# TensorE's side work in front of the flips of probabilities in an attention loop

## The chip, the cores and the metric

The kernel runs on one core of one Trainium2 chip. The metric is the device time of one execution in microseconds (us).

## The reference, cut to what matters

Four batches of 512 tokens with 512 features go through a small cross attention, an attention block with a mixture of 8 experts, a second cross attention and a second mixture of 32 experts. The attention block, in which the change lies, computes for normed x of shape 4 x 512 x 512:

```
kv_d, q_d = x @ kv_d_w, x @ q_d_w                    # 512 -> 128
k_p, q_p, v = kv_d @ k_u_w, q_d @ q_u_w, kv_d @ v_u_w
k_r, q_r = rope(x @ rope_k_w), rope(q_d @ rope_q_w)
k, q = concat(k_p, k_r), concat(q_p, q_r)            # 16 heads of 32
probs = softmax(causal(q @ k.T / sqrt(32)))
h = x + (probs @ v) @ o_w
```

Then `rmsnorm(h)` goes to a router (7 logits a token, two experts chosen) and to the first mixture.

## The kernel before

The function `front` holds the attention block. Each engine has its own program, written out in order by hand; they meet only through semaphores. A loop over 128 steps n (four batches b of 32 steps s) does the attention. A step is one pair of heads and one tile of 128 queries. Steps 0 to 15 of a batch take query tiles 1 and 0 in turn, with 256 and 128 keys (narrow steps); steps 16 to 31 take tiles 3 and 2, with 512 and 384 keys (wide steps). A narrow step is one unit with both heads, `(n, None)`; a wide step is two units, `(n, 0)` and `(n, 1)`, one head each. There are 192 units.

For a unit, TensorE computes the scores (L1092) and adds the causal mask (L1093); VectorE takes the row maxima (`maxima`, L869); ScalarE takes the exponentials (`exponents`, L739); TensorE transposes these probabilities block by block (`flip_probs`, L1134) into PSUM bank 4, or bank 5 for a second head of a wide step; bank 4 is copied to `prob_t` by VectorE (`prob_t_first`, L876) and bank 5 by ScalarE (`prob_t_second`, L748); TensorE multiplies with the values for two steps at a time (`attend`, L1112). TensorE runs the scores two units ahead. `take(bank, name, n)` makes TensorE wait until the last user of a PSUM bank has been copied out, in program order of the `take` calls.

With each step goes a piece of work for the neighbouring batches, `between(b, s)`, on TensorE, ScalarE and VectorE alike. For the batch to come: flips of its normed input and the down projections (steps 0 to 4), `plain` (L1154, L1155), `turned` (L1160, L1162) and `values` (L1168) for token tiles 0 and 1 at steps 6 to 8 and for tiles 2 and 3 at steps 14, 15 and 18 to 21, and the flips of queries and keys (L1082) at steps 9, 12 and 22 to 28. VectorE rotates the result of `turned` (`rotate`, L933 to L940) and forms the low parts of queries and keys (L917, L923); ScalarE copies the results out (L764, L770, L777, L782). For the batch done: the output projection (`output`, L1185; steps 0, 1, 3, 5), flips of its normed rows (steps 10, 11, 13) and the router's `logits` (L1198; steps 12, 14, 15). In the last batch, steps 20 and 24 hold an `output` of that batch itself. Steps 16, 17, 23, 25 and 27 have nothing for TensorE.

The order of work that matters here: TensorE does, for each unit, scores of the unit two ahead, `attend`, flips of denominators, the flip of this unit's probabilities, then `between`. VectorE does maxima of the next unit, then the copy of the last flip and the last step's `between`. ScalarE does this unit's exponentials, then the copy of the last second-head flip and the last step's `between`.

Of the kernel before, what the change touches and what calls it, by code (L numbers as in the profile page):

```python
# [42 lines left out]
NS = len(STEPS)  # L43
# [500 lines left out]
def front(nc, a, m, c, dram, s_init):  # L544
    ctx = ExitStack()
    with ctx:
# [70 lines left out]
        def copied_first(n):  # L617

            b, s = divmod(n, NS)
            return b * (NS + PHASE) + (s + 1 + min(s + 1, PHASE))  # L620

        def copied_second(n):
            b, s = divmod(n, NS)
            return b * PHASE + max(0, s + 1 - PHASE)
# [444 lines left out]
        def _(pe):  # L1069
# [4 lines left out]
            def take(bank, name, n):  # L1074

                if bank in emptied and emptied[bank] != (name, n):
                    pe.wait_ge(S[emptied[bank][0]], emptied[bank][1])
                emptied[bank] = (name, n)
# [44 lines left out]
            def flip_probs(n, e):  # L1123
                i, u = STEPS[n % NS][0], n % 2
                bank = 5 if e == 1 else 4
                pe.wait_ge(S["pexp"], 2 * n + heads_of(n, e)[-1] + 1)
                if e == 1:
                    take(5, "ptb", copied_second(n))
                else:
                    take(4, "pta", copied_first(n))  # L1130
                for e in heads_of(n, e):
                    for j in range(i + 1):
                        at = block_of(n, e, j) % TPB * P
                        last = tr(ps[:, bank, at:at + P], prob[:, u, e, j * P:(j + 1) * P], ident)  # L1134
                last.then_inc(S["pt"], 1 if is_wide(n) else 2)

            def z_flip(b, t):
                pe.wait_ge(S["z"], b * TPB + t + 1)
                take(BANK["zt"][t], "zts", b * TPB + t + 1)
                four(BANK["zt"][t], z[:, t, :]).then_inc(S["zt"], 1)  # L1140

            def down(b, w, name, out, bank):
                pe.wait_ge(S["zts"], TPB * (b + 1))
                take(bank, out, b + 1)
                for k in range(DC):
                    last = mm(ps[:, bank, :], w[:, k, :], z_t[:, k, :], start=(k == 0), stop=(k == DC - 1))
                last.then_inc(S[name], 1)

            def plain(b, t):
                q, bank = slice(t * P, (t + 1) * P), BANK["pp"][t]  # L1150
                pe.wait_ge(S["kvds"], b + 1)
                pe.wait_ge(S["qds"], b + 1)
                take(bank, "qkp", b * TPB + t + 1)
                mm(ps[:, bank, 0:256], q_d[:, q], w_q[:, 0:256], start=True, stop=True)  # L1154
                mm(ps[:, bank, 256:512], kv_d[:, q], w_ku[:, :], start=True, stop=True).then_inc(S["pp"], 1)  # L1155

            def turned(b, t):
                q = slice(t * P, (t + 1) * P)
                take(3, "qkr", b * TPB + t + 1)
                mm(ps[:, 3, 0:256], q_d[:, q], w_q[:, 256:512], start=True, stop=True)  # L1160
                for k in range(DC):
                    last = mm(ps[:, 3, 256:512], z_t[:, k, q], w_kr[:, k, :], start=(k == 0), stop=(k == DC - 1))  # L1162
                last.then_inc(S["pr"], 1)

            def values(b, t):
                pe.wait_ge(S["kvds"], b + 1)
                take(BANK["v"][t], "vs", b * TPB + t + 1)
                mm(ps[:, BANK["v"][t], :], kv_d[:, t * P:(t + 1) * P], w_vu[:, :], start=True, stop=True).then_inc(S["pv_"], 1)  # L1168

            def queries_flip(b, t):  # L1170
                pe.wait_ge(S["qkp"], b * TPB + t + 1)
                pe.wait_ge(S["qkr"], b * TPB + t + 1)
                take(BANK["tq"][t], "qls", b * TPB + t + 1)
                four(BANK["tq"][t], qk[:, t % 2, 0:HEADS, :].rearrange("p h e -> p (h e)")).then_inc(S["tq"], 1)

            def keys_flip(b, t):
                take(BANK["tk"][t], "kls", b * TPB + t + 1)
                four(BANK["tk"][t], qk[:, t % 2, HEADS:2 * HEADS, :].rearrange("p h e -> p (h e)")).then_inc(S["tk"], 1)

            def output(b, n):  # L1180
                t, bank = QUERY_ORDER[n], OUT_BANK(b, n)
                pe.wait_ge(S["attd"], b * TPB + n + 1)
                take(bank, "hres", b * TPB + n + 1)
                for k in range(DC):
                    last = mm(ps[:, bank, :], att_t[:, t, k, :], w_o[:, k, :], start=(k == 0), stop=(k == DC - 1))  # L1185
                last.then_inc(S["oproj"], 1)

            def hidden_flip(b, t):
                pe.wait_ge(S["hn"], b * TPB + t + 1)
                take(BANK["hnt"][t], "hnts", b * TPB + t + 1)  # L1190
                four(BANK["hnt"][t], h[:, t, :]).then_inc(S["hnt"], 1)
# [9 lines left out]
            def ranks(b):  # L1201
                pe.wait_ge(S["masked"], b + 1)
                take(3, "slotted", b + 1)
                places(nc, r, MOE0, c, m, m["before0"], 3).then_inc(S["ranked"], 1)

            def between(b, s):

                done, then = b - 1, b + 1
                if then < BATCH and s in (0, 1):
                    z_flip(then, 2 * s)  # L1210
                    z_flip(then, 2 * s + 1)
                if done >= 0:
                    if s in (0, 1):
                        output(done, s)
                    if s in (3, 5):
                        output(done, (s + 1) // 2)
                if then < BATCH:
                    if s == 2:
                        down(then, w_kvd, "kvd", "kvds", BANK["kvd"])
                    if s == 4:  # L1220
                        down(then, w_qd, "qd", "qds", BANK["qd"])
                    if s in (6, 7):
                        plain(then, s - 6)
                    if s in (6, 8):
                        turned(then, s // 2 - 3)
                        values(then, s // 2 - 3)
                    if s in (9, 12):
                        queries_flip(then, s // 3 - 3)
                        keys_flip(then, s // 3 - 3)
                if done >= 0:  # L1230
                    if s == 10:
                        hidden_flip(done, 0)
                    if s == 11:
                        hidden_flip(done, 1)
                        hidden_flip(done, 2)
                    if s == 12:
                        logits(done, 0)
                        logits(done, 1)
                    if s == 13:
                        hidden_flip(done, 3)  # L1240
                    if s in (14, 15):
                        logits(done, s - 12)
                if then < BATCH:
                    if s in (14, 15):
                        values(then, s - 12)
                    if s in (18, 20):
                        plain(then, s // 2 - 7)
                    if s in (19, 21):
                        turned(then, s // 2 - 7)
                    if s in (22, 26):  # L1250
                        queries_flip(then, s // 4 - 3)
                    if s in (24, 28):
                        keys_flip(then, s // 4 - 4)
                if b == LAST and s in (20, 24):
                    output(LAST, s // 4 - 5)
                if done >= 0 and s == 30:
                    ranks(done)
# [17 lines left out]
            for at in range(len(UNITS) + 4):  # L1275
                if at + 2 < len(UNITS):
                    n, e = UNITS[at + 2]
                    for e in heads_of(n, e):
                        scores(n, e)
                if at >= 2 and at - 2 < len(UNITS):  # L1280
                    n, e = UNITS[at - 2]
                    if n % 2 == 1 and e != 0:
                        attend(n - 1)
                for n in at_unit["den_flip"].get(at, ()):
                    denominators(n)
                if at < len(UNITS):
                    n, e = UNITS[at]
                    flip_probs(n, e)
                    if e != 0:
                        between(n // NS, n % NS)  # L1290
            for n in range(2, TPB):
                output(LAST, n)
# [1002 lines left out]
```

## Time and profile before

| | |
|---|---|
| median of 3 runs | 1813.83 us (1813.83 to 1819.98) |
| the profiled execution's own time | 1829.46 us |
| its span, first to last instruction | 1827.3 us |
| attention loop in it | 138.5 to 575.0 us |
| TensorE busy in the span | 87% |
| VectorE busy | 74% |
| ScalarE busy | 57% |
| GpSimd busy | 43% |

The shares are means over a span of which the attention loop is a quarter; the mixtures fill most of the rest. PE is TensorE's matmul side, PEld its weight loads, DVE VectorE, ACT ScalarE, POOL GpSimd, SP SyncE. A wait in square brackets at the end of a line is the engine's idle time just before it, and what ended it.

### The profile page before, as it was taken

How to read it: one execution, taken by the hardware profiler on the slowest of the kernel's cores; microseconds unless marked ns; L12 is line 12 of the kernel's file. 1: busy time of each engine (PE TensorE's matmuls, PEld its weight loads, DVE VectorE, ACT ScalarE, POOL GpSimd, SP SyncE). 2: the span in 40 equal slices, each digit the busy share in tenths (PEclk: the TensorE clock that was granted, in tenths of full speed). 3: DMA queues.
4: the chain of work that ended last, by engine and by line, in shares of the span. 5: the costliest groups of instructions: out<-in, count | busy, mean ns of one | idle time of the engine just before them, and what ended most of it. 6: DMA issues, size and time to landing. Idle time of an engine off the chain costs nothing. (4 is left out here: it accounts for less than half of the span.)

```text
span 1827.3 us, 34273 instructions
## 1 busy us (share of the span) xinstructions
PE 1591.3 (87%) x8854; PEld 1198.3 (66%) x8855; DVE 1358.6 (74%) x2777; ACT 1038.2 (57%) x1969; POOL 792.2 (43%) x547
## 2 busy tenths in 40 slices
PE   4578898899887799999968927999999999999991
PEld 2446666666564577777736526888888878788880
DVE  6836866766675477666639776999999999899992
ACT  1124635535343366666524215888888888888870
POOL 5100010210202323545410124788788888788881
PEclk9589998998999799999978557999999999999996
DMA  9225435443350544765574314988888889898778
GB/s 332 85 73 140 90 89 142 92 123 65 70 139 1 165 158 136 173 137 100 85 218 152 118 59 91 215 184 184 181 200 172 187 187 210 210 223 181 130 121 302
DMA packets 169997, 270.56 MB, mean 148 GB/s; under 512 B 20416, under 2 KB 96192, under 8 KB 168192
## 3 DMA queue, kind: packets, MB, share of 16 engines
q0 software_dynamic: 49008, 117.24, 32.4%
q1 hardware_dynamic: 120896, 152.18, 28.5%
q8 instruction: 46, 0.75, 0.2%
q14 instruction: 47, 0.39, 0.1%
HBM read 153.72 MB, written 89.06 MB: 133 GB/s over the span
## 5 line engine op out<-in xcount | busy, mean ns | idle before, releaser
L1636 DVE TENSOR_TENSOR moe_w_lo<-moe_w_up,moe_w_hi 128x1536 fp32r<-128x1536 f32 (+1 forms) x216 | 408.4, 1891 | 10.1 <-ACT moe_w_hi L1515 7.8
L1515 ACT ACTIVATE moe_w_hi<-moe_w_up 128x1536 fp32r (+3 forms) x216 | 343.4, 1590 | 7.9 <-issue 7.9
L1456 POOL DMA_INDIRECT moe_rows<-moe_rows,moe_ids x200 | 316.4, 1582 | 67.2 <-issue 56.4
L1731 PE MATMUL psum<-moe_w_hi,moe_rows_hi 128*128 128x384 f32 (+1 forms) x864 | 322.4, 373 | 3.3 <-DVE moe_rows_lo L1630 3.3
L1733 PE MATMUL psum<-moe_w_hi,moe_rows_lo 128*128 128x384 f32 (+1 forms) x864 | 304.4, 352 | 0.0
L1732 PE MATMUL psum<-moe_w_lo,moe_rows_hi 128*128 128x384 f32 (+1 forms) x864 | 304.3, 352 | 0.0
L1757 PE MATMUL psum<-moe_w_down,moe_hid_t 128*128 (+1 forms) x544 | 268.9, 593 | 1.9 <-DVE moe_tail_t L1624 1.3
L1472 POOL DMA_INDIRECT moe_sum<-moe_res,moe_ids x100 | 167.2, 1672 | 98.3 <-ACT moe_res L1558 54.4
L1472 POOL DMA_INDIRECT moe_other<-moe_res,moe_ids x100 | 169.7, 1697 | 85.4 <-ACT moe_res L1558 33.4
L1630 DVE TENSOR_TENSOR moe_rows_lo<-psum,moe_rows_hi 128x512 fp32r<-128x512 f32 x216 | 148.9, 689 | 51.0 <-issue 40.5
L739 ACT ACTIVATE prob<-psum,neg_top 128x128 f32<-128x128 f32 (+3 forms) x256 | 133.1, 528 | 88.4 <-DVE neg_top L869 78.5
L1731 PEld LDWEIGHTS psum<-moe_w_hi,moe_rows_hi 128*128 128x128 f32 x864 | 164.0, 190 | 11.3 <-DVE moe_rows_lo L1630 4.2
L1733 PEld LDWEIGHTS psum<-moe_w_hi,moe_rows_lo 128*128 128x128 f32 x864 | 163.5, 189 | 9.4
L1732 PEld LDWEIGHTS psum<-moe_w_lo,moe_rows_hi 128*128 128x128 f32 x864 | 164.4, 190 | 7.4
L869 DVE TENSOR_REDUCE neg_top<-psum 128x1 f32<-128x128 f32 (+3 forms) x256 | 117.3, 482 | 54.3 <-PE psum L1093 52.7
L1532 ACT ACTIVATE moe_gate<-psum 128x192 f32<-128x192 f32 (+1 forms) x216 | 73.4, 340 | 143.1 <-PE psum L1733 137.4
L1501 ACT ACTIVATE moe_rows_hi<-psum 128x512 fp32r<-128x512 f32 x216 | 130.5, 604 | 25.3 <-PE psum L1712 25.0
L1652 DVE TENSOR_TENSOR moe_hid<-moe_gate,psum 128x192 f32<-128x192 f32 (+1 forms) x216 | 79.0, 366 | 86.5 <-ACT moe_gate L1532 86.4
L1526 ACT ACTIVATE moe_tail_hi<-moe_w_down 128x512 fp32r (+1 forms) x160 | 101.1, 632 | 70.9 <-issue 67.8
L1134 PE MATMUL psum<-const_sb,prob 128*128 128x128 f32 x640 | 112.1, 291 | 31.3 <-ACT prob L739 27.9
L1712 PE MATMUL psum<-const_sb,moe_rows 128*128 128x128 f32 x864 | 131.2, 275 | 7.1 <-DMA moe_rows<-moe_rows,moe_ids 5.3
L1762 PE MATMUL psum<-moe_tail_hi,moe_tail_t 128*128 128x512 f32 x160 | 127.2, 795 | 0.0
(285 smaller groups left out, 2885.8 us busy)
## 6 DMA issues: line engine op xcount, KB each, us to landing
moe_w_up<-in_L_ffn_w_gate SPq DMA_DIRECT2D x32, 384.0 KB
moe_w_up<-in_L_ffn_w_up SPq DMA_DIRECT2D x32, 384.0 KB
q_st<-q_hi SPq DMA_DIRECT2D x64, 128.0 KB, 2.8
k_st<-k_hi SPq DMA_DIRECT2D x64, 128.0 KB, 3.0
k_st<-k_lo SPq DMA_DIRECT2D x64, 128.0 KB, 3.1
q_st<-q_lo SPq DMA_DIRECT2D x64, 128.0 KB, 3.1
moe_w_down<-in_L_ffn_w_down SPq DMA_DIRECT2D x32, 256.0 KB
moe_w_down<-in_L_ffn_w_down SPq DMA_DIRECT2D x64, 128.0 KB
```

Source lines behind the costliest of these rows:

```text
L739: sc.activation(prob[:, u, e, 0:(i + 1) * P], score_at(n, e, (i + 1) * P), ACT.Exp, bias=neg_top[:, u, e:e + 1], accum_out=den[:, i, 2 * h ...
L1456: pool.indirect_dma_start(rows[u][:, :], None, d["rows"], bass.IndirectOffsetOnAxis(ids[:, t:t + 1], 0)).then_inc(gathered[u], 16)
L1472: pool.indirect_dma_start(sums[t % 2], bass.IndirectOffsetOnAxis(ids[:, t:t + 1], 0), res[t % RESULTS][:, :], None, compute_op=ALU.add).th ...
L1501: sc.activation(rows_hi[i][:, :], ps[:, i, :], ACT.Copy).then_inc(T["rth"], 1)
L1515: sc.activation(w_hi[u % SPLITS][:, :], w_up[:, bass.ds(at * DC, DC), :].rearrange("p a n -> p (a n)"), ACT.Copy).then_inc(T["wh"], 1)
L1630: v.tensor_tensor(rows_lo[i][:, :], ps[:, i, :], rows_hi[i][:, :].bitcast(F32), ALU.subtract).then_inc(T["rts"], 1)
L1636: v.tensor_tensor(w_lo[u % SPLITS][:, :], w_up[:, bass.ds(at * DC, DC), :].rearrange("p a n -> p (a n)"), w_hi[u % SPLITS][:, :].bitcast(F ...
L1712: last = tr(ps[:, i, k * P:(k + 1) * P], rows[u][:, k * P:(k + 1) * P], ident)
L1731: mm(ps[:, 2 + i, 0:2 * I], hi, w_h, start=(k == 0), stop=False)
L1732: mm(ps[:, 2 + i, 0:2 * I], hi, w_l, start=False, stop=False)
L1733: last = mm(ps[:, 2 + i, 0:2 * I], lo, w_h, start=False, stop=(k == DC - 1))
L1757: done = mm(ps[:, 5 + i, :], hid_t[i][:, j, :], tile_at(w_down, at * n_fc + j), start=(j == 0), stop=(j == n_fc - 1))
```

## The change

TensorE's `between(b, s)` is issued in front of the flip of that step's probabilities in steps 6 to 9 and 14 to 28, and behind it, as before, in steps 0 to 5, 10 to 13 and 29 to 31. The programs of the other engines are the same; the number of instructions is the same.

```
                 if at < len(UNITS):
                     n, e = UNITS[at]
+                    early = e != 0 and n % NS in (6, 7, 8, 9, 14, 15, 16, ..., 28)
+                    if early:
+                        between(n // NS, n % NS)
                     flip_probs(n, e)
-                    if e != 0:
+                    if e != 0 and not early:
                         between(n // NS, n % NS)
```

(The list in the code names each of the steps 6 to 9 and 14 to 28.)

## Rows read from the trace of the kernel before

**Rows 1.** Windows of the attention loop, one a batch: their sum.
```profile
sum 436.50, PE 389.26 PEld 281.52 DVE 301.19 ACT 212.02 POOL 34.83; mean PE 97.32 PEld 70.38 DVE 75.30 ACT 53.01 POOL 8.71
```

**Rows 2.** Waits of TensorE in the loop: total us, times, longest.
```profile
PE psum L1134 <- ACT prob L739: 27.9, 46, 2.5
...
PE psum L1134 <- DVE prob_t L876: 3.1, 4, 2.0
```

**Rows 3.** Timeline, batch 0, steps 18 and 19: start us, us, engine, line.
```profile
193.00 0.66 PE L1134 MATMUL psum<-const_sb,prob 128*128 128x128 f32 x4 [0.31 <-ACT prob L739]
...
195.77 0.55 PE L1134 MATMUL psum<-const_sb,prob 128*128 128x128 f32 x3 [0.31 <-ACT prob L739]
...
196.15 0.60 PE L1160 MATMUL psum<-w_q,q_d 128*128 128x256 f32 x2
...
198.13 0.53 PE L1092 MATMUL psum<-k_st,q_st 128*128 128x384 f32 x1
...
198.52 0.69 DVE L933 TENSOR_TENSOR rot_a<-psum,const_sb 128x512 f32<-128x512 f32 x1 [1.90 <-PE psum L1162]
```

**Rows 4.** TensorE's timeline, batch 0 step 21 and batch 1 step 19.
```profile
203.49 0.55 PE L1134 MATMUL psum<-const_sb,prob 128*128 128x128 f32 x3 [0.63 <-ACT prob L739]
...
309.48 0.55 PE L1134 MATMUL psum<-const_sb,prob 128*128 128x128 f32 x3 [0.53 <-ACT prob L739]
...
311.02 0.55 PE L1134 MATMUL psum<-const_sb,prob 128*128 128x128 f32 x3 [0.68 <-ACT prob L739]
```

**Rows 5.** Timeline, batch 0, steps 24 and 25.
```profile
214.51 0.66 PE L1134 MATMUL psum<-const_sb,prob 128*128 128x128 f32 x4
...
215.00 0.60 PE L1082 MATMUL psum<-const_sb,qk 128*128 128x128 f32 x4
215.20 0.60 ACT L748 ACTIVATE prob_t<-psum 128x512 f32<-128x512 f32 x1 [0.56 <-PE psum L1134]
...
215.69 0.59 ACT L782 ACTIVATE k_hi<-psum 128x512 fp32r<-128x512 f32 x1
...
216.17 0.58 ACT L739 ACTIVATE prob<-psum,neg_top 128x384 f32<-128x384 f32 x1
...
216.90 0.33 PE L1134 MATMUL psum<-const_sb,prob 128*128 128x128 f32 x1 [0.35 <-ACT prob L739]
```

**Rows 6.** Timeline, batch 1, steps 6 to 10.
```profile
266.56 0.68 DVE L876 COPY prob_t<-psum 128x512 f32<-128x512 f32 x1
...
267.55 0.69 DVE L933 TENSOR_TENSOR rot_a<-psum,const_sb 128x512 f32<-128x512 f32 x1 [0.31 <-PE psum L1162]
...
267.80 0.62 PE L1092 MATMUL psum<-k_st,q_st 128*128 128x128 f32 x1
...
276.70 0.41 DVE L876 COPY prob_t<-psum 128x256 f32<-128x256 f32 x1
...
277.26 0.41 PE L1134 MATMUL psum<-const_sb,prob 128*128 128x128 f32 x2 [0.33 <-DVE prob_t L876]
```

**Rows 7.** Windows in batches 1 and 3: busy us of each engine, clock, DMA.
```profile
267.55:277.11 9.56, 9.38 (x74) 7.06 (x72) 9.49 (x24) 5.32 (x18) 0.00 (x0) 1.00 0.94 264
306.00:332.00 26.00, 22.08 (x225) 17.19 (x216) 22.09 (x64) 15.04 (x41) 0.00 (x0) 1.00 0.36 83
...
288.00:292.00 4.00, 4.00 (x17) 3.36 (x16) 1.97 (x4) 1.11 (x5) 0.00 (x0) 0.50 0.77 192
...
520.00:524.00 4.00, 4.00 (x42) 3.40 (x41) 3.01 (x7) 2.19 (x8) 0.00 (x0) 1.00 0.90 226
```

**Rows 8.** Timeline, flips of steps 14 and 16, batches 1 and 3.
```profile
288.13 0.42 PE L1134 MATMUL psum<-const_sb,prob 128*128 128x128 f32 x1
...
299.30 0.42 PE L1134 MATMUL psum<-const_sb,prob 128*128 128x128 f32 x1
...
521.04 0.63 PE L1134 MATMUL psum<-const_sb,prob 128*128 128x128 f32 x4
...
525.78 0.42 PE L1134 MATMUL psum<-const_sb,prob 128*128 128x128 f32 x1
```

More of the change, by code:

```diff
@@ L1287, in _ @@
                     n, e = UNITS[at]
+                    early = e != 0 and n % NS in (6, 7, 8, 9, 14, 15, 16, 17, 18, 19, 20, 21, 22, 23, 24, 25, 26, 27, 28)
+                    if early:
+                        between(n // NS, n % NS)
                     flip_probs(n, e)
-                    if e != 0:
+                    if e != 0 and not early:
                         between(n // NS, n % NS)
```

## The prediction

> **What bounds the kernel now.** I began with the windows of the attention loop, one for each batch, and their sum [rows 1]. The loop is 436.5 us of the 1827.3 us span, and everything behind it (two mixtures of experts and the layer between them) is untouched by the edit. So the edit can act on a quarter of the kernel. In it TensorE is busy 389.3 us, VectorE 301.2, ScalarE 212.0: TensorE paces the loop, and time can be won only where TensorE idles.
>
> The list of waits says how much that is [rows 2]: in front of flips of probabilities (L1134) TensorE waits 27.9 us for ScalarE's exponentials, in 46 places, and 3.1 us in 4 places for VectorE's copy of the previous flip. I then went along TensorE's timeline and gave each of these stalls to its step. They are not where the moved work is, for the most part. 8.1 us are in batch 3's first half (steps 3, 5, 7, 9), which moves nothing. In the second halves, stalls stand at the second-head flips of steps 18, 19, 21, 23, 25, 27, 29 and at first-head flips of 18, 19, 23 and 24. TensorE's `between` is empty at 16, 17, 23, 25, 27; at 22, 24, 26 and 28 it has work, but the flip that it passes does not wait.
>
> **What the change removes.** It adds and drops no instruction. It issues TensorE work ahead of the flip it used to follow: `plain`, `turned`, `values`, `logits`, query and key flips, two `output`s. No DMA, and nothing of SyncE's or GpSimd's queues, moves; what those queues wait for (scores, `qls`, `kls`) comes within 2 us of its old time, and neither is late for TensorE in these steps.
>
> A stall is filled where a moved block stands at a stalling flip. Step 18: 0.31 us [rows 3]. Step 19: 0.31 in batch 0 [rows 3], 0.68 in batch 1 [rows 4] and the same in batch 2. Step 21: 0.63 [rows 4]. The blocks take 0.7 us (`plain`) to 2.0 (`turned`: from its first product at 196.15 to the next scores at 198.13 [rows 3]), so each covers its stall. Sum: batch 0 0.31 + 0.31 + 0.63 = 1.25, batches 1 and 2 0.31 + 0.68 + 0.63 = 1.62 each, together **4.5 us**. Batch 3 has no such blocks.
>
> Not all of it stays. In batches 1 and 2 the flip after step 18's waits 0.53 us for exponentials whose maxima queue behind VectorE's routing work [rows 4]; TensorE comes there 0.31 earlier and waits 0.31 longer. Given back: 2 x 0.31 = **0.6 us**.
>
> One thing is added to the gain. VectorE's rotation (L933) waits 1.90 us for `turned` [rows 3], and the next maxima, and so the next exponentials, queue behind it. With `turned` ahead of the flip, it also ends earlier by the time of a three-block flip, 196.15 - 195.77 = 0.38 us. After step 21 that lead shows in the stall of step 23 (0.68), which nothing else fills. I take 3 x 0.37 = **1.1 us**; its bounds are 0 and that.
>
> **What the change costs, second half.** The flip that is now behind the block is read by ScalarE, in order: copy of the flip (L748), copy of the query or key flip, then the exponentials of the next step's second head, for which TensorE waits. Rows 5 show this chain closed at step 24: flip 214.51, copy 215.20, key copy 215.69, exponentials 216.17, next second flip 216.90 after a stall of 0.35 us [rows 5]. The stall is there before the change, so the chain, not TensorE's work, sets this stretch. Each microsecond by which the flip is late is a microsecond. With the four key transposes first, the flip starts 215.00 - 214.51 = 0.49 later but without its first-load gap, so it ends about 0.43 later (I use the difference of the ends, 215.60 - 215.17). Between 0 and the 0.60 of the row I take 0.43. This holds for steps 24, 26 and 28 of three batches (at 22 the stall that follows is set by VectorE, which hides it): 9 x 0.43 = **3.9 us lost**. VectorE is not the cover here; it gets slack.
>
> For the two `output`s of batch 3 (steps 20 and 24, eight products of 512 columns) the same chain ends about when TensorE arrives, since the next scores must come behind the `output` either way: 0, at most 0.1.
>
> The Trainium skill, "TensorE: Matmul & The Clock Gate", section "Step-by-step: what each phase is for", says that matmuls keep their program order and only weight loads are pulled ahead. By that rule a matmul behind a blocked flip cannot fill its stall by itself, and reordering by hand is the only way; the trace agrees with its stalls, during which ready work stands behind. It would make the gain the 4.5 us above, and says nothing of the chain behind the flip.
>
> **What it costs, first half.** No moved flip waits there, so nothing is won. But here the flips of all steps use one bank, emptied by VectorE (L876), and before the change the block stands between two flips and hides that copy. After it, only the scores do where the next step isn't moved. That place is step 9 to step 10. In batch 1 the flip of step 10 waits 0.33 us for the copy already [rows 6]. And the copy comes later: flip 6 now ends where the next scores start, at 267.80, so its copy (0.68 us, at 266.56 before) starts at about 267.95, and the rotation, which is behind it, at 268.65 instead of 267.55 [rows 6]. VectorE is 1.1 us late there, and from there to 277.11 it is busy 9.49 of 9.56 us [rows 7], so it cannot catch up. The copy of flip 9 (276.70 and 0.41 long [rows 6]) ends at 278.2 instead of 277.1, and TensorE resumes at 278.4 instead of 277.26. That is **1.15 us each in batches 1 and 2**. What is late next: `hidden_flip`, then the query flips, all behind that flip in TensorE's queue; nothing there gives it back. Batch 0 has no residual or norm work on VectorE, so only the bare copy shows: 0.3 (bounds 0 and 1.15). In batch 3 step 15's `logits` go first, and the flip of the denominators (at unit 16) waits for the bank of the logits, which VectorE empties behind its copy of flip 15; at full clock that is 0.25 (0 to 0.4), in batches 1 and 2 it hides in TensorE's half clock. Together **2.9 us lost**.
>
> **The sum.** -4.5 + 0.6 - 1.1 + 3.9 + 2.9 = **+1.8 us**. The profiled execution took 1829.46 us with its span of 1827.3, so it becomes 1831.3. The runs have a median of 1813.83, so I give **1815.6 us**. With the low ends (no chain, no bank loss): -4.5 + 0.6 - 1.1 = -5.0, 1808.8. With the high ends (chain 9 x 0.60 = 5.4, no lead from the rotation, banks 3 x 1.15 + 3 x 0.4 = 4.7): +6.2, 1820.0.
>
> **Rivals.**
> *Pure filling.* The stalls are filled and neither chain nor bank gives back: 1808.8 us, -0.3%. For it: stalls of 0.3 to 0.7 us at moved flips. Against it: the 0.35 at step 25 is unfilled and chained.
> *Nothing comes of it.* TensorE's total is the same and each filled stall opens again at the next unmoved flip: 1813.8 us. For it: step 18 and its follower in batches 1 and 2.
> *Slower by the clock.* In batch 1, steps 14 to 16, the granted clock is 0.50 (the lower level, 1.2 GHz), after a step in which TensorE had sat idle for VectorE [rows 7]. From the flip of step 14 to that of step 16 it takes 299.30 - 288.13 = 11.2 us, in batch 3 at full clock 4.7 [rows 8]; with about 1.5 for the two `values` that batch 3 lacks, a fall costs 5 us. The new stall of over 1 us at step 10 could bring it on four steps earlier, in both batches: 2 x 5 + 1.8 = +11.8, **1825.6 us**, slower. It decides from two further falls; one gives 1820.6, within the noise. Against: in batch 0 steps 1 to 28 have single stalls of 2.0 us, and batch 3 steps 3 to 9 stalls of 1.2 to 2.5, and only some are followed by a low clock.
> The same skill page, section "A second HAM failure mode: psum-queue depth-cycling", says that short idles between groups of matmuls that cycle through PSUM banks can throttle and release the clock again and again. By it the time would be this rival's; here the second halves have such idles at every odd step and their clock stays at 1.00 (306 to 332 us [rows 7]), so this trace doesn't agree for idles under 1 us.
> *Faster by the clock.* The blocks of steps 14 and 15 (matmuls of 512 columns) now run ahead of their flips, and the half-clock stretches of batches 1 and 2 end or vanish: 1.8 - 10 = -8.2, 1805.6 us; with pure filling beside it, past the bound.
>
> **Numbers.** 0.5%, 9 us, is about what a measurement of this kernel tells from no change; the runs before lie 6 us apart. Chances: the forecast 0.50, pure filling 0.14, nothing 0.13, slower by the clock 0.13, faster by the clock 0.10. Of the slower rival 0.11 lies past the bound (one fall only does not), of the forecast 0.02, so slower 0.13; faster 0.09 (0.07 of the clock's, 0.02 of filling); same 0.78. The range reaches from the faster clock case to the slower one, without their tails: 1806 to 1825 us. The forecast's own range is 1809 to 1820.
>
> **What would show it.** Right: in the loop's waits, L1134 on L739 falls by 1 to 2 us only: the stalls of steps 18, 19 and 21 gone, those of steps 25, 27 and 29 grown from 0.35 to about 0.8; L1134 on VectorE's copy up from 3.1 to some 5.5 us, at step 10; scores of step 22 earlier by about 1 us within the batch, the end of the batch not. Wrong: step 25's stall unchanged (the chain has slack that I don't see), step 10's unchanged, or a changed count of 4-us windows with the clock at 0.50.

## The result and the profile after

Over 19 runs each, the changed kernel took a median of 1821.52 us (1813.33 to 1831.2), the kernel before 1815.54 us (1805.98 to 1821.53). The ratio is **1.0038, interval 1.002 to 1.0055**: 3.6 to 10 us slower, 6.9 in the middle, and within the 0.5% that the prediction called no change. Forecast was +1.8 us. The profiled execution after took 1813.33 us with a span of 1811.1, less than that of before, although the kernel is slower over the runs. Single executions scatter by more than the effect: from flip 0 to flip 5 of batches 2 and 3, where nothing is moved, the one before took 32.4 and 25.1 us and the one after 26.5 and 19.3, which is 11.7 us. So the stretches between two flips of the same batch are compared below, not spans.

The waits of TensorE in the loop after the change (total us, times, longest), to be set beside [rows 2]:

```profile
PE psum L1134 <- ACT prob L739: 24.7, 34, 2.0
PE psum L1134 <- DVE prob_t L876: 6.6, 5, 2.0
...
PE psum L1160 <- ACT qk L770: 0.9, 4, 0.2
```

The exponentials are waited for in 34 places instead of 46, 24.7 us instead of 27.9. Of these 3.2 us, 2.5 are in batch 3's first half (steps 3, 5, 7 and 9, 8.1 us before and 5.6 after), where nothing is moved; the moved steps and what follows them account for 0.7. What VectorE's copy costs has doubled, from 3.1 us to 6.6. The third row is a wait that was not among those of before: `turned` waits for ScalarE's copy of `plain`.

Batch 0, steps 18 and 19 after the change, on TensorE, beside [rows 3]:

```profile
198.07 0.70 PE L1160 MATMUL psum<-w_q,q_d 128*128 128x256 f32 x2 [0.23 <-ACT qk L770]
...
200.33 0.49 PE L1134 MATMUL psum<-const_sb,prob 128*128 128x128 f32 x3
```

The flip of step 19's second head stands behind `turned` and waits no more (0.31 before). In front of `turned` (L1160) there is now 0.23 us. `turned` uses the bank that `plain` filled a step earlier and ScalarE empties; before, the flip of step 19's second head lay between as well, now `turned` comes ahead of it and ScalarE is not through.

Steps 24 and 25 of batch 0, beside [rows 5]:

```profile
216.29 0.66 PE L1082 MATMUL psum<-const_sb,qk 128*128 128x128 f32 x4
...
216.78 0.60 PE L1134 MATMUL psum<-const_sb,prob 128*128 128x128 f32 x4
...
217.42 0.60 ACT L748 ACTIVATE prob_t<-psum 128x512 f32<-128x512 f32 x1 [0.99 <-PE psum L1134]
...
217.91 0.59 ACT L782 ACTIVATE k_hi<-psum 128x512 fp32r<-128x512 f32 x1
...
218.39 0.58 ACT L739 ACTIVATE prob<-psum,neg_top 128x384 f32<-128x384 f32 x1
...
219.12 0.44 PE L1134 MATMUL psum<-const_sb,prob 128*128 128x128 f32 x2 [0.79 <-ACT prob L739]
```

The key flip (L1082) is first, then the flip of the probabilities; ScalarE's copy of that flip (L748) starts 217.42 - 216.29 = 1.13 us after the first of the two, before 215.20 - 214.51 = 0.69. The difference is 0.44 us, and the stall of the next second flip went from 0.35 to 0.79.

Steps 6 to 10 of batch 1, beside [rows 6]:

```profile
271.19 0.69 DVE L876 COPY prob_t<-psum 128x512 f32<-128x512 f32 x1 [1.86 <-issue]
...
271.80 0.68 DVE L933 TENSOR_TENSOR rot_a<-psum,const_sb 128x512 f32<-128x512 f32 x1
...
280.95 0.42 DVE L876 COPY prob_t<-psum 128x256 f32<-128x256 f32 x1
...
281.51 0.63 PE L1134 MATMUL psum<-const_sb,prob 128*128 128x128 f32 x4 [1.24 <-DVE prob_t L876]
```

VectorE stands idle for 1.86 us in front of the copy of flip 6 (`issue` means that the profile names nothing it waited for; in the kernel the copy waits for that flip, which is now behind the block). The rotation starts right behind that copy, and the flip of step 10 waits 1.24 us instead of 0.33.

The clock in windows of the same length as two of [rows 7]:

```profile
292.00:296.00 4.00, 4.00 (x14) 2.60 (x13) 0.69 (x1) 1.30 (x5) 0.00 (x0) 0.50 0.56 174
306.00:332.00 26.00, 22.54 (x204) 17.69 (x203) 23.08 (x66) 15.28 (x41) 0.00 (x0) 1.00 0.33 76
```

In these rows the third number from the end is the granted clock. The wide steps keep the full clock (1.00) although their stalls changed; the fall behind step 13 (0.50) is still there.

The stretches from the start of one flip (L1134) to that of another, in us, worked out from the timelines of all kernels. The first pair of flips are those of steps 5 and 10, the second those of steps 16 (first head) and 31 (second head); in each cell batches 0, 1 and 2.

| kernel | flip 5 to flip 10 | flip 16 to flip 31 |
|---|---|---|
| before | 14.3, 17.5, 17.5 | 46.2, 49.7, 48.4 |
| the change | 16.3, 19.1, 19.1 | 46.2, 49.3, 48.8 |
| only step 9 | 14.7, 17.5, 17.5 | not moved |
| only steps 6, 7, 8 | 16.3, 19.1, 19.1 | not moved |
| narrow steps only | 16.3, 19.1, 19.1 | 46.3, 49.5, 48.4 |
| only steps 18 to 21 | 14.3, 17.5, 17.5 | 45.3, 48.4, 47.3 |
| only steps 22 to 28 | 14.3, 17.5, 17.5 | 47.1, 50.4, 49.9 |
| steps 18 to 28, ScalarE's swap | 14.3, 17.5, 17.5 | 45.3, 48.4, 47.3 |
| the change, VectorE's swap | 14.8, 18.5, 18.6 | 46.2, 49.3, 48.8 |
| the change, both swaps | 14.8, 18.5, 18.5 | 45.3, 48.8, 47.4 |

(Batch 1 of the kernel before still had some half clock at the start of the second stretch; where it had none, the unmoved stretch reads 49.5. In the two kernels marked "not moved", batch 0 reads 47.6 in it, with a mean granted clock of 0.94 from flip 22 to flip 31, and batch 1 of the last row had a fall at its end.) Where no part of one of these stretches is moved, it reads the same from kernel to kernel within 0.1 us as long as the clock is full, so differences of 0.3 us are to be read here, which no total time shows.

### The profile page after: what moved, and what is told of

It reads as the page before. It is cut to its first block and busy times, and to the rows that moved or that the text cites. A ratio compares the mean times of both kernels' runs of the same rounds, so it can differ in the third digit from the quotient of the medians.

```text
span 1811.1 us, 34273 instructions
## 1 busy us (share of the span) xinstructions
PE 1570.2 (87%) x8854; PEld 1185.4 (65%) x8855; DVE 1359.4 (75%) x2777; ACT 1041.4 (58%) x1969; POOL 787.9 (44%) x547
## 5 line engine op out<-in xcount | busy, mean ns | idle before, releaser
L1459 POOL DMA_INDIRECT moe_rows<-moe_rows,moe_ids x200 | 324.3, 1622 | 67.2 <-issue 56.4
L1475 POOL DMA_INDIRECT moe_sum<-moe_res,moe_ids x100 | 164.6, 1646 | 98.4 <-ACT moe_res L1561 49.5
L1475 POOL DMA_INDIRECT moe_other<-moe_res,moe_ids x100 | 163.8, 1638 | 87.5 <-ACT moe_res L1561 30.3
L1734 PEld LDWEIGHTS psum<-moe_w_hi,moe_rows_hi 128*128 128x128 f32 x864 | 163.7, 189 | 11.7 <-DVE moe_rows_lo L1633 4.5
L1134 PE MATMUL psum<-const_sb,prob 128*128 128x128 f32 x640 | 108.8, 285 | 31.3 <-ACT prob L739 24.7
```

Source lines behind the costliest of these rows:

```text
L1459: pool.indirect_dma_start(rows[u][:, :], None, d["rows"], bass.IndirectOffsetOnAxis(ids[:, t:t + 1], 0)).then_inc(gathered[u], 16)
L1475: pool.indirect_dma_start(sums[t % 2], bass.IndirectOffsetOnAxis(ids[:, t:t + 1], 0), res[t % RESULTS][:, :], None, compute_op=ALU.add).th ...
L1734: mm(ps[:, 2 + i, 0:2 * I], hi, w_h, start=(k == 0), stop=False)
```

## The experiments

Each kernel differs from the changed one in the list of steps whose block goes in front, and some in an order on another engine. "Before" in a ratio is the kernel before the change on the same chip.

**Step 9 alone, and steps 6 to 8 alone.** The loss in the narrow steps had two explanations: VectorE late from the copy of flip 6 on, or the bank alone.

```
-                    early = e != 0 and n % NS in (6, 7, 8, 9, 14, 15, 16, ..., 28)
+                    early = e != 0 and n % NS in (9, 99)
```

> Only step 9's block (query and key flips of token tile 0) goes in front of its flip; all other steps as before the change. Theory (VectorE's lateness): the loss at step 10 comes from the late copy of flip 6, behind which the rotation and all later VectorE work slip; that copy is not moved here, so the flip of step 10 waits 0.3 to 0.6 us for VectorE's copy in batches 0 to 2, as before (0 and 0.33), and from the flip of step 5 to that of step 10 it takes 14.3 us in batch 0 and 17.6 in batch 1, as before, within 0.4. Rival (the bank alone): the loss comes from the missing block between flips 9 and 10, so the wait at step 10 is 1.1 to 1.3 us as after the full change, and the stretch is 1 us longer.

```
+                    early = e != 0 and n % NS in (6, 7, 8)
```

> Only steps 6, 7 and 8 have their blocks in front; step 9's block stands behind its flip again. Theory (VectorE's lateness): VectorE is 1.1 us late from the copy of flip 6 on, so the copy of flip 9 is late and the flip of step 10 waits about 1.2 us although step 9's block stands between the flips; flip 5 to flip 10 takes 16.3 us in batch 0 and 19 in batch 1, as after the full change. Rival (the bank alone): the wait is back at 0 to 0.33 us and the stretch at 14.3 and 17.6 us.

The flip of step 10 in batch 1 with step 9 alone moved:

```profile
278.54 0.41 PE L1134 MATMUL psum<-const_sb,prob 128*128 128x128 f32 x2 [0.33 <-DVE prob_t L876]
```

The copy of flip 9 and the flip of step 10 in batch 1 with steps 6 to 8 moved:

```profile
282.21 0.41 DVE L876 COPY prob_t<-psum 128x256 f32<-128x256 f32 x1
...
282.77 0.30 PE L1134 MATMUL psum<-const_sb,prob 128*128 128x128 f32 x1 [1.06 <-DVE prob_t L876]
```

With only step 9 moved the wait is 0.33 us, as before; with steps 6 to 8 moved and step 9 behind its flip it is 1.06, and the stretch is as long as after the full change to 0.1 us in all three batches. Batch 0 with step 9 alone got 0.4 us longer, with a wait of 0.23. So the loss is VectorE's lateness; the missing cover between the flips is worth 0.4 us in one batch. (Each of these two has a single run, so no ratio.)

**The parts of the second half, timed.** Steps 18 to 21 fill stalls; steps 22 to 28 should only lengthen ScalarE's chain.

```
+                    early = e != 0 and n % NS in (18, 19, 20, 21)
```

> Only steps 18 to 21 have their blocks in front (plain and turned of tiles 2 and 3, and the output of the last batch at step 20). Theory: the stalls of 0.31 to 0.68 us at steps 18, 19 and 21 go, nothing in the steps 22 to 29 is given back (the stalls at steps 25, 27 and 29 stay 0.35 us), and flip 16 to flip 31 takes 1.0 to 1.7 us less in each of batches 0 to 2; in all 3.5 to 5 us faster than the kernel before, ratio 0.997 to 0.998. Rival (the filled stalls open again behind them): no change, 1.000, and the stretch from flip 16 to flip 31 within 0.3 us of 46.2, 49.7 and 48.5 us.

```
+                    early = e != 0 and n % NS in (22, 24, 26, 28)
```

> Only the blocks of steps 22, 24, 26 and 28 go in front (query and key flips of tiles 2 and 3, and the last batch's second output). Theory (ScalarE's chain): the stalls at steps 25, 27 and 29 grow from 0.35 to 0.79 us in batches 0 to 2, step 23's stays or grows by up to 0.4; flip 16 to flip 31 is 1.3 to 1.8 us longer in these batches; 4 to 5 us slower, ratio 1.002 to 1.003. Rival (VectorE paces these steps and hides it): stretch and time as before.

Steps 18 to 21: ratio 0.9952 (0.9921 to 0.9983). Flip 16 to flip 31 is 0.9, 1.1 and 1.1 us shorter (against 49.5 in batch 1), 3.1 in all (a little under the expected 3.5 to 5), and the stalls at steps 25, 27 and 29 stay at 0.35. Steps 22 to 28: ratio 0.999 (0.9961 to 1.0019), which does not show the loss: the expected 1.002 to 1.003 lies just above the interval. The stretches show it: 0.9, 0.9 and 1.5 us longer, 3.3 in all, or 1.0018, where 1.3 to 1.8 a batch were expected. The flip of step 25's second head in batch 0:

```profile
217.39 0.44 PE L1134 MATMUL psum<-const_sb,prob 128*128 128x128 f32 x2 [0.79 <-ACT prob L739]
```

**ScalarE's order turned round.** If the chain is what costs, ScalarE should copy the two flips in the order in which TensorE now makes them.

```
+                    swap = e == 1 and n % NS in (22, 24, 26, 28)
+                    if swap:
+                        between(n // NS, n % NS)
                     if e == 1:
                         prob_t_second(n)
-                    if e != 0:
+                    if e != 0 and not swap:
                         between(n // NS, n % NS)
```

with the blocks of steps 18 to 28 in front and those of the narrow steps behind.

> The blocks of steps 18 to 28 go in front, those of steps 6 to 15 stay behind; and in steps 22, 24, 26 and 28 ScalarE copies the query or key flip out before it copies the flip of probabilities, the order in which TensorE now makes them. Theory (ScalarE's chain): the 0.79 us stalls at steps 25, 27 and 29 go back to 0.35 to 0.4, since the copy of the query or key flip fills the time until the late flip; flip 16 to flip 31 is 1.0 to 1.7 us shorter than before the change in batches 0 to 2; 3.5 to 5 us faster in all, ratio 0.997 to 0.998. Rival (the stall is TensorE's own, by the position of the flip): the stalls stay near 0.79 us and the whole is within 1 us of before.

Steps 24 and 25 of batch 0 in this kernel (L1085 is the key flip, L1137 the flip of probabilities, L782 the key copy, L748 the other):

```profile
213.23 0.66 PE L1085 MATMUL psum<-const_sb,qk 128*128 128x128 f32 x4
...
213.72 0.60 PE L1137 MATMUL psum<-const_sb,prob 128*128 128x128 f32 x4
213.92 0.60 ACT L782 ACTIVATE k_hi<-psum 128x512 fp32r<-128x512 f32 x1 [0.56 <-PE psum L1085]
...
214.42 0.59 ACT L748 ACTIVATE prob_t<-psum 128x512 f32<-128x512 f32 x1
...
214.90 0.58 ACT L739 ACTIVATE prob<-psum,neg_top 128x384 f32<-128x384 f32 x1
...
215.62 0.44 PE L1137 MATMUL psum<-const_sb,prob 128*128 128x128 f32 x2 [0.35 <-ACT prob L739]
```

The key copy starts 213.92 - 213.23 = 0.69 us after the first flip, as the other copy did in [rows 5]; the stall is 0.35 us again, at all of steps 25, 27 and 29. The stretches are those of steps 18 to 21 alone. Ratio 0.9956 (0.9923 to 0.9988).

**The narrow part, timed.**

```
+                    early = e != 0 and n % NS in (6, 7, 8, 9, 14, 15)
```

> Only the blocks of the narrow steps 6 to 9, 14 and 15 go in front. Theory: the whole loss of the change is here: flip 5 to flip 10 is 1.5 to 2 us longer in batches 0 to 2, flip 16 to flip 31 as before within 0.3 us; 4 to 7 us slower, ratio 1.002 to 1.004. Rival (the loss is in the second halves, or in the mixtures behind): ratio 0.999 to 1.001.

Ratio 1.0034 (1.0007 to 1.006), 6.2 us, with 2.0 + 1.6 + 1.6 = 5.2 us of it from flip 5 to flip 10. This is nearly the whole loss of the change.

**VectorE's order turned round.** VectorE copies a flip first and then does the step's own work. With the block in front, the work is ready first.

```
+                swap = 1 <= at <= len(UNITS) and UNITS[at - 1][1] is None and UNITS[at - 1][0] % NS in (6, 8, 15)
+                if swap:
+                    n = UNITS[at - 1][0]
+                    between(n // NS, n % NS)
                 if 1 <= at <= len(UNITS) and UNITS[at - 1][1] != 1:
                     prob_t_first(UNITS[at - 1][0])
...
-                if 1 <= at <= len(UNITS) and UNITS[at - 1][1] != 0:
+                if 1 <= at <= len(UNITS) and UNITS[at - 1][1] != 0 and not swap:
                     between(n // NS, n % NS)
```

> The full change, and in steps 6, 8 and 15 VectorE does its own work of the step (rotation, sum of the logits) before it copies the flip of probabilities, the order in which TensorE now makes them. Theory (VectorE's lateness): the idle 1.9 us of VectorE in front of the copy of flip 6 goes, the wait at step 10 falls from 1.15 to 1.24 us to 0.3 to 0.6, flip 5 to flip 10 is back at 14.3 us in batch 0 and 17.6 in batch 1 within 0.5, the wait of the denominators for the logits (0.3 to 0.5) goes; 4 to 6 us faster than the changed kernel, which is within 1 us of the kernel before, ratio 0.999 to 1.001. Rival (the loss has another cause, such as the bank alone): wait and stretch stay, ratio 1.003 to 1.004.

VectorE in batch 0 at step 6, the rotation now in front of the copy:

```profile
163.89 0.69 DVE L933 TENSOR_TENSOR rot_a<-psum,const_sb 128x512 f32<-128x512 f32 x1 [2.32 <-PE psum L1166]
...
165.95 0.68 DVE L876 COPY prob_t<-psum 128x512 f32<-128x512 f32 x1
```

Ratio 1.0 (0.9973 to 1.0027). The wait at step 10 is 0.23 us in all three batches, below what was expected. The stretch fell to 14.8, 18.5 and 18.6. Of the loss, 0.5 of 2.0 us remained in batch 0 and 1.0 of 1.6 in batches 1 and 2, in these more than expected. The trace shows a new wait in these two, in batch 1 at the flip of step 9:

```profile
276.85 0.68 DVE L876 COPY prob_t<-psum 128x512 f32<-128x512 f32 x1
...
277.68 0.41 PE L1138 MATMUL psum<-const_sb,prob 128*128 128x128 f32 x2 [0.77 <-DVE prob_t L876]
```

The copy of flip 8 now stands behind the rotation of step 8, and the flip of step 9 needs its bank: 0.77 us, which no kernel without this swap has. So the swap at step 8 takes back part of what it gives; the swap at step 6 alone was not tried. The wait of the denominators for the logits is gone, as expected. From flip 13 to flip 16 of batch 0 it is 6.0 us as after the change, so that part didn't move either.

**Both swaps.** The full change with the swaps of the two engines.

> The full change, with VectorE's swap of steps 6, 8 and 15 and ScalarE's swap of steps 22, 24, 26 and 28. Theory: both losses go and the filled stalls of steps 18 to 21 stay; 3 to 5 us faster than the kernel before, ratio 0.997 to 0.998. Rival: at most one of the swaps acts, ratio 0.999 or more.

Ratio 0.9968 (0.9942 to 0.9993), the stalls as in the two kernels before. It is faster than the kernel before, as expected, but more than its stretches say; see below.

**Steps 14 and 15 alone.**

```
+                    early = e != 0 and n % NS in (14, 15)
```

> Only the blocks of steps 14 and 15 go in front. Theory (two small waits of their own): values of step 14 waits 0.2 us for the query's low part and the first wide flips come later by the bank of the denominators, so from flip 13 to flip 16 it is 0.6 us longer in batch 0 (6.0 instead of 5.4) and flip 5 to flip 10 is as before (14.3, 17.5, 17.5). Rival (they are a consequence of VectorE being late from step 6): flip 13 to flip 16 of batch 0 is 5.4 us.

Flip 13 to flip 16 of batch 0 is 6.0 us (5.4 before), flip 5 to flip 10 as before, so these two steps lose 0.6 us by themselves. TensorE at `values` of step 14:

```profile
181.22 1.10 PE L1168 MATMUL psum<-w_vu,kv_d 128*128 128x512 f32 x2 [0.23 <-DVE q_lo L917]
```

It waits for the bank that held the query flip of step 12, emptied in VectorE's work of step 13. Before the change the flip of step 14 lay over that wait.

**The three best, on one chip.**

> The same as the kernel with only steps 18 to 21 in front, now beside the other two on one chip. By the stretches of its profile it is 3.2 us shorter than the kernel before: ratio 0.998, interval around it. If the first ratio of 0.995 was more than scatter: 0.995 to 0.997.

> Steps 18 to 28 in front with ScalarE's swap, beside the other two on one chip. Its stretches were those of the kernel with steps 18 to 21 alone within 0.1 us, so the ratio is the same as that one's within 0.002: 0.998 by the stretches.

> The full change with both swaps, beside the other two on one chip. By the stretches (narrow steps 0.5 to 1.0 us a batch longer than before, wide ones 0.9 to 1.1 shorter) it is within 1 us of the kernel before: ratio 0.999 to 1.000, and 2 to 3 us behind the other two. If its first ratio of 0.997 holds, the narrow steps give something that the stretches do not show, such as fewer falls of the clock.

Ratios 0.9984 (0.9961 to 1.0006), 0.9975 (0.9951 to 0.9998) and 0.9962 (0.9935 to 0.9989). The three intervals overlap, so they show no order; the medians on that chip, 12 runs each, are 1813.7, 1812.0 and 1806.3 us. The first agrees with its stretches (3.1 us, 0.998); its earlier 0.9952 has that in its interval, as has the 0.9956 of the second. The full change with both swaps was 0.997 and 0.996, twice, where its stretches give 2.5 + 0.6 - 2.7 = +0.4 us. Much of that goes with the clock. Every run has its granted clock, averaged over the whole span; the means over the runs are:

| kernel | its mean clock | before, same chip |
|---|---|---|
| the change, both swaps | 0.9233 | 0.9191 |
| the same, again | 0.9230 | 0.9186 |
| steps 18 to 28, ScalarE's swap | 0.9218 | 0.9171 |
| the same, again | 0.9188 | 0.9186 |
| only steps 18 to 21 | 0.9192 | 0.9171 |
| the same, again | 0.9183 | 0.9186 |
| only steps 22 to 28 | 0.9203 | 0.9191 |
| narrow steps only | 0.9183 | 0.9191 |
| the change, VectorE's swap | 0.9196 | 0.9191 |

The standard error of each difference is about 0.001. The kernel with both swaps ran at a clock 0.004 higher on both its chips. The one with ScalarE's swap alone did so on its first chip, where its ratio of 0.9956 was also below its stretches, and not on the second, where the ratio agreed with them. Among the runs of the kernel before on the two chips of the first two rows, 0.004 more of clock goes with 4.6 and 6.5 us less of time, about what the stretches leave open (6 to 7 us). Flip 13 to flip 16 of batches 1 and 2 in the kernel with both swaps (length, busy times, granted clock after the GpSimd column):

```profile
285.70:295.89 10.19, 8.93 (x56) 5.97 (x55) 4.98 (x12) 3.51 (x10) 0.00 (x0) 0.83 0.70 181
399.64:408.21 8.57, 7.31 (x56) 5.20 (x55) 4.88 (x12) 3.40 (x10) 0.00 (x0) 1.00 0.60 147
```

and in the kernel before:

```profile
285.00:299.30 14.30, 13.04 (x56) 9.16 (x55) 5.48 (x12) 3.62 (x10) 0.00 (x0) 0.54 0.80 202
408.50:422.70 14.20, 12.94 (x56) 9.06 (x55) 5.43 (x12) 3.52 (x10) 0.00 (x0) 0.52 0.54 115
```

Both profiles of the version with both swaps read 10.2 and 8.6 us for the two stretches. The same stretch, with none of its work moved, in the kernel with steps 18 to 21:

```profile
284.17:292.52 8.35, 7.09 (x57) 5.10 (x55) 5.08 (x12) 3.06 (x9) 0.00 (x0) 1.00 0.78 247
397.57:409.13 11.56, 10.30 (x56) 7.31 (x55) 5.17 (x12) 3.05 (x9) 0.00 (x0) 0.70 0.60 148
```

So this stretch alone takes 8.35 us at full clock and 14.3 at about half, and which it is changes from one execution to the next. So its 24 runs show that the kernel with both swaps ran at a higher clock; that the clock falls less behind step 13 rests on two profiles, and why this order of work should do that is not shown.

## Why the prediction was right, and where it was off

**The number.** The measured median of 1821.5 us lies in the stated range of 1806 to 1825, but above the forecast's own range of 1809 to 1820, and the difference of 6.9 us is above even its high end of +6.2. The wide range was there for two clock rivals that did not come. So "no change beyond 0.5%" was right, but not because the sum was: it was off by 5 us, and the bound of 9 us had room for that.

**Fills, right in kind, too large.** The stalls at steps 18 (second head), 19 and 21 went, and in batches 1 and 2 the flip behind step 18 opened again, from 0.53 to 0.86 us in batch 1: the 0.31 that was said, as 0.33. But from flip 16 to flip 22 only 0.6, 0.75 and 0.75 us were won in the three batches, 2.1 together, where 4.5 - 0.6 = 3.9 were forecast. Of the missing 1.8, 0.9 is a wait that I had not seen: `turned` waits 0.23 us in front of itself, twice in batch 0 and once each in batches 1 and 2. I asked which inputs a moved block needs and not what bank its neighbour block had left full. The other 0.9 is not accounted for.

**The lead of the rotation, right in size, at another stall.** The term was 1.1 us, 0.37 a batch, and was looked for in step 23's second-head stall. That one stayed at 0.68 with steps 18 to 21 moved. But the first-head stall of the same step (0.20, 0.49, 0.21) became 0, 0.16 and 0, and from flip 22 to flip 31, where this kernel moves nothing, each of the three batches is 0.32 us shorter. In batch 0 the rotation starts 1.83 us ahead of the second-head flip of step 22 before the change and 2.16 with steps 18 to 21 moved, 0.33 more. Net gain of steps 18 to 21: 3.1 us where the terms give 4.5 - 0.6 + 1.1 = 5.0.

**ScalarE's chain, right in kind and size.** 0.44 us a step where 0.43 was said, at steps 24, 26 and 28. Three batches lose 0.9, 0.9 and 1.5, together 3.3 us against 3.9. The stalls grow by 0.44 in all three, but the distance from the flip of step 25 to that of step 27 grows from 5.03 us to 5.33 in batches 0 and 1 and from 4.90 to 5.33 in batch 2: in the first two it was 0.13 longer already before. That the swap on ScalarE restores 0.35 shows the cause.

**VectorE's lateness in the narrow steps: the mechanism right, the term mis-sized, and this is the main step that made the loss too small.** I gave 1.15 us each to batches 1 and 2 and 0.3 to batch 0, on the ground that batch 0 "has no residual or norm work on VectorE". It lost most, 2.0 us. Flip 5 and the first rotation of batch 0 before the change:

```profile
159.78 0.44 PE L1134 MATMUL psum<-const_sb,prob 128*128 128x128 f32 x2
...
164.84 0.69 DVE L933 TENSOR_TENSOR rot_a<-psum,const_sb 128x512 f32<-128x512 f32 x1 [2.11 <-PE psum L1162]
```

Batch 0, flip 5 to flip 10, after the change:

```profile
160.00 0.44 PE L1134 MATMUL psum<-const_sb,prob 128*128 128x128 f32 x2
...
166.02 0.69 DVE L876 COPY prob_t<-psum 128x512 f32<-128x512 f32 x1 [3.67 <-issue]
...
166.63 0.68 DVE L933 TENSOR_TENSOR rot_a<-psum,const_sb 128x512 f32<-128x512 f32 x1
...
168.82 0.70 PE L1160 MATMUL psum<-w_q,q_d 128*128 128x256 f32 x2 [0.29 <-DVE qk L940]
...
172.63 0.69 DVE L876 COPY prob_t<-psum 128x512 f32<-128x512 f32 x1 [2.47 <-issue]
...
173.24 0.68 DVE L933 TENSOR_TENSOR rot_a<-psum,const_sb 128x512 f32<-128x512 f32 x1
...
175.69 0.42 DVE L876 COPY prob_t<-psum 128x256 f32<-128x256 f32 x1
...
176.26 0.30 PE L1134 MATMUL psum<-const_sb,prob 128*128 128x128 f32 x1 [1.15 <-DVE prob_t L876]
```

VectorE is idle 3.67 us in front of the copy of flip 6 and 2.47 in front of that of flip 8. Both times the rotation has to start behind the copy. The first starts 166.63 - 160.00 = 6.63 us after flip 5, where before it was 164.84 - 159.78 = 5.06. The second starts 13.24 instead of 11.07 us after it, 2.2 late, and both times the rotation is needed soon: `turned` of step 8 waits 0.29 for it, and the flip of step 10 waits 1.15 for the copy of flip 9. That a busy VectorE can't catch up holds in batches 1 and 2; in batch 0 it cannot catch up either, though it is idle, since it is idle in front of the wrong instruction. The Trainium skill ("TensorE: Matmul & The Clock Gate", section "Architectural detail: the array is 16× 32×32, not 1× 128×128") says that ScalarE and VectorE take their instructions strictly in order. The trace agrees: during the idle 3.67 us nothing behind the copy was started, though `turned`'s last product had ended at 164.6, 1.4 us before the copy.

In batches 1 and 2 the loss was 1.6 each where 1.15 was said. The rotation of batch 1 starts 9.37 us after flip 5 instead of 7.81, so VectorE is 1.56 us late there and not 1.1, and it is still 1.56 late at the copy of flip 9. The forecast let flip 6 end where the row of the next scores starts (267.80) and its copy start at 267.95, which is 8.2 us after flip 5; it started 8.76 after it.

**The banks at steps 14 to 16, half right.** The wait of the denominators for the logits came (0.30 us in batch 1, 0.51 in batches 2 and 3). It does not hide in the half clock of batches 1 and 2, as was said. Another one, `values` for the query flip's bank, had not been named; with what follows it is 0.6 us in batch 0. In the kernel with steps 14 and 15 alone, batch 2 ran from flip 13 to flip 16 at full clock in 9.1 us, where unmoved kernels at full clock take 8.3; batch 3 took 5.9, unmoved 5.5 at full clock. These two steps cost more than the 0.25 us that they had in the sum.

**The sum.** By the stretches: 5.2 (flips 5 to 10) + 0.6 (flips 13 to 16 in batch 0) - 3.1 + 3.3 = +6.0 us, to which steps 14 and 15 add 0.4 in each of batches 1 and 2 at half clock, 0.8 at full, and 0.4 in batch 3: some 7 to 8 us; measured +6.9 (3.6 to 10). The forecast of +1.8 lies below the interval. The measured 0.38% is within the 0.5% forecast, though the interval reaches a little beyond it.

**The rivals.** Pure filling fell: both losses are there. That nothing comes of it fell too. Slower by the clock: the new stalls of 1.2 us at step 10 brought no fall there; the narrow steps' loss of 5.2 us is made at full clock, since the stretch reads the same in every kernel that has it. Faster by the clock fell for the change itself: the kernel with the narrow steps alone, which has nearly the whole loss, had a mean clock of 0.9183 against 0.9191. The falls behind step 13 are one part of what scatters the runs. Another is flip 0 to flip 5 of batches 2 and 3, 26.5 to 32.4 and 19.3 to 25.9 us with nothing moved there, in part at full clock (29.6 us at 1.00 in batch 2 of the kernel with steps 18 to 21); what makes it is open.

Left open: 0.9 us of the fills, 0.3 to 0.5 us a batch of what VectorE's swap leaves from flip 5 to flip 10, and why the full change with both swaps ran at a higher clock.

## What to carry to other kernels

Work moved in front of a stalling instruction fills the stall, but the instruction's readers get it later: on each engine that reads it, look at what stands behind that read in its queue, and turn the order round there too (here it brought the stretches of the full change from +6.0 to +0.4 us; the ratio went from 1.004 to 0.997, the rest of which goes with a higher clock). Do so for idle engines as well; here VectorE was idle for 3.67 us at the head of its queue and 1.6 us late behind it. Then look at what the turned order makes late: VectorE's swap at step 8 brought a new wait of 0.77 us at step 9. And move blocks only where the flip in their way really waits: of 19 steps in the list, four (18 to 21, tried only together) did the good.

## What the runs showed of the hardware

That a stretch of some 8 us, with one and the same work, runs at granted clock 1.00 in one batch or execution and at 0.54 in another, 8.35 us or 14.3. That is 6 us of scatter in one batch, nearly as much as the whole effect of the change. The idle in its first part does not decide it: in batches 1 and 2 of all 14 profiles TensorE waits the same 1.26 us there, up to 1.7 us behind flip 13, whether the stretch then runs at full clock, at half or in between.
